# Linear attention in a deeper pipeline with scores in four row groups, and softmax attention with values of two tiles in one run, probabilities scaled by VectorE and scores of heads two and two

## The chip, the cores and the metric

The kernel runs on one core of a Trainium2 chip. Its time is the device time of one launch in microseconds (us), the median of three runs. The engines of the core are named as the profile names them: PE (TensorE; PEld is its loading of weights), DVE (VectorE), ACT (ScalarE), POOL (GpSimd) and SP (the queue of DMAs).

## What is computed

Two layers on x of shape (2, 1024, 256), in fp32. The first is linear attention with 16 heads of 16 features, computed in pieces of 64 positions by the reference (in tiles of 128 by the kernel). The second is a block of causal softmax attention (32 query heads, 8 key/value heads of 64) and a mixture of 8 experts, two for each token.

```
x = x + layernorm(linear_attention(layernorm(x)))
    # q, k: products of two feature maps; s = tril(q k^T); o = s v + q (sum of k^T v so far); o / rms(o)
y = layernorm(x)
h = y + attention(rmsnorm(y))        # softmax(q k^T / 8, causal) v, then wo
x = x + layernorm(h + moe(rmsnorm(h)))
```

## The kernel before

Each engine has its program written out by hand, in order, and semaphores join them: an engine that waits holds up everything behind it on that engine. Three stages follow each other.

**Stage 1, linear attention.** `pair_step(s, front, back)` works on tile s of both batches at once, 128 positions each, 8 tiles. Its front part turns normalised x (`xn` to `xnT`), makes four feature maps (L1109), q and k, the values, and the masked scores of tile s (`score`, L1120). Its back part, in the next step, makes the output of the tile before (L1131 state part, L1133 score part, in four column groups of 32), its rms, the projection `ao` (L1177), two layernorms and `rT_all`. For the scores the heads share 128 partitions, 16 each: POOL (L457) and ACT (L582) copy q eight times, each copy masked to one head (`qx`), and PE multiplies all 128 rows of k with 512 columns of them. DVE multiplies the result with the triangle (`mask`, L774).

**Stage 2, softmax attention.** A sequence is one key/value head of one batch; there are 16, and each has 8 query tiles of 128 (t is the tile's number over all, 128 in all; below c = t modulo 8, so tile c has w = 128(c+1) keys and c+1 blocks of 128 keys). For each tile and each of its four query heads PE makes scores (`score`, L1285 and L1286, two passes in fp32r), DVE adds the causal mask, writes the result to `probs` and takes the row maximum (`maximum`, L884), ACT exponentiates and sums (`exponent`, L640). In the next step PE transposes the probabilities block by block (L1301, four heads to a block, into three PSUM banks used in turn, `TURNS`), and ACT and DVE take turns in copying the blocks out (`evacuate_part`, L648 and L892). One step later `values` (L1313) multiplies them with the values into `bank[2]`, in two column groups. The row sums are turned to the other layout by a copy on POOL (`spread`, L500) and two transposes (L1298); DVE divides by them when it takes the output (`oT`, L909). Then comes `project_out` (L1322) and the sum into `acc` (L922). `project` makes one of six slices of keys, values and queries (L1253) or a transpose of the values (L1243) at the end of each step; ACT and DVE split its result (L630 to L634, and `low_part`, L872 and L877).

**Stage 3** routes the tokens and runs 39 slots of experts (L1401, L1410).

The order of stage 2 on PE is this, for each t from 0 on (`third` splits the blocks of a tile in three parts):

```
score(t,0)  values(t-2)  score(t,1)  turn_part(t-1,0)  score(t,2)  turn_part(t-1,1)
project_out(t-2)  score(t,3)  turn_part(t-1,2)  project(item_of(t))
```

## Time and profile before

| | |
|---|---|
| median of 3 runs | 1934.72 us (1933.41 to 1934.87) |
| the profiled execution: its time, its span | 1933.22 us, 1931.3 us |
| busy in the span: PE, PEld, DVE, ACT, POOL | 94%, 74%, 55%, 48%, 14% |
| TensorE clock granted, mean | 0.976 of full speed |
| chain that ended last: PE, DVE, ACT | 86%, 7%, 2% |

The span runs from the first to the last instruction. A matmul's row gives its whole duration, and following matmuls begin before it ends, so the pace of PE is read from the starts of two rows.

### The profile page before, as it was taken

What the parts mean: (1) busy time and instruction counts of PE and PEld (TensorE: products, weight loads), DVE (VectorE), ACT (ScalarE), POOL (GpSimd) and SP (SyncE); (2) the same over time, 40 slices, a digit from 0 to 9 for tenths busy, and PEclk for the clock granted to TensorE, in tenths of its full rate; (3) what the DMA queues carried; (4) which work ended last, traced back from release to release, by engine and by line L of the source; (5) the groups of instructions that cost most, each with busy time, mean ns of one, the idle gap of its engine ahead of it and who ended that gap; (6) DMA issues with size and microseconds to landing.
All of it is one profiled execution on the core that took longest, in us unless ns stands there. A gap on an engine that the chain in (4) does not pass through costs nothing.

```text
span 1931.3 us, 32217 instructions
## 1 busy us (share of the span) xinstructions
PE 1813.6 (94%) x12286; PEld 1428.7 (74%) x12286; DVE 1055.0 (55%) x2465; ACT 924.1 (48%) x2049; POOL 261.1 (14%) x355
## 2 busy tenths in 40 slices
PE   6999689999999999999999999999985999999994
PEld 5666457777777777777777777777765999999993
DVE  3666556766776766767767667667655111111112
ACT  3343255655656656656656656656651222222223
POOL 2222110000000000000000000000001222222222
PEclk9999889999999999999999999999986999999997
DMA  2000010000000000000000000000017134213443
GB/s 83 0 0 0 0 44 1 9 1 1 9 1 1 9 1 1 10 1 1 9 1 1 9 1 1 1 1 1 23 34 245 22 92 128 48 26 87 119 125 95
DMA packets 46042, 60.02 MB, mean 31 GB/s; under 512 B 8944, under 2 KB 39536, under 8 KB 45936
## 3 DMA queue, kind: packets, MB, share of 16 engines
q1 hardware_dynamic: 36336, 46.16, 7.2%
q0 software_dynamic: 7536, 10.36, 3.2%
q10 hardware_dynamic: 2064, 2.10, 0.3%
q8 instruction: 66, 1.08, 0.2%
q14 instruction: 40, 0.33, 0.1%
HBM read 138.43 MB, written 11.40 MB: 78 GB/s over the span
## 4 chain that ended last, share of the span: by engine, by line
PE 86%; DVE 7%; ACT 2%; issue 2%; POOL 1%; DMA 1%; SPq 0%; DVEq 0%; POOLq 0%; ACTq 0%
PE wide L1401 15%; PE bank L1313 13%; PE bank L1301 12%; PE bank L1253 9%; PE wide L1285 8%; PE bank L1410 7%; PE wide L1286 7%; PE bank L1322 6%; PE wide L1120 2%; PE bank L1109 2%; PE bank L1298 1%; ACT qhl L634 1%; PE bank L1177 1%; DVE arena L802 1%; PE bank L1243 1%
## 5 line engine op out<-in xcount | busy, mean ns | idle before, releaser
L884 DVE CUSTOM_DVE_ANT_0 arena<-wide,arena 128x896 f32<-128x896 f32 (+7 forms) x512 | 383.8, 755 | 223.2 <-PE wide L1286 219.3
L640 ACT ACTIVATE arena<-arena,nmax 128x896 f32<-128x896 f32 (+7 forms) x512 | 397.0, 776 | 177.3 <-DVE nmax L884 174.2
L1285 PE MATMUL wide<-khi,qhl 128*128 128x512 f32 (+3 forms) x768 | 346.3, 452 | 1.7 <-DVE qhl L877 1.7
L1301 PE MATMUL bank<-ident,arena 128*128 128x128 f32 x2304 | 308.5, 274 | 0.0
L648 ACT COPY arena<-bank 128x512 f32<-128x512 f32 (+1 forms) x352 | 191.7, 545 | 214.0 <-PE bank L1301 206.3
L1401 PEld LDWEIGHTS wide<-wo,arena 128*128 128x128 f32 x2496 | 287.0, 193 | 3.2 <-issue 1.3
L1401 PE MATMUL wide<-wo,arena 128*128 128x128 f32 x2496 | 287.3, 277 | 0.9 <-ACT wo L693 0.9
L1313 PE MATMUL bank<-arena,vt 128*64 128x256 f32 x2304 | 277.0, 385 | 0.0
L1301 PEld LDWEIGHTS bank<-ident,arena 128*128 128x128 f32 x2304 | 262.3, 141 | 16.6 <-issue 0.4
L1286 PE MATMUL wide<-klo,qhl 128*128 128x512 f32 (+3 forms) x768 | 256.0, 347 | 0.0
L1050 DVE TENSOR_TENSOR wo<-wide,wo 128x512 f32<-128x512 f32 x78 | 53.9, 692 | 368.1 <-PE wide L1401 368.1
L892 DVE COPY arena<-bank 128x512 f32<-128x512 f32 (+1 forms) x352 | 222.9, 639 | 9.2 <-PE bank L1301 8.4
L1313 PEld LDWEIGHTS bank<-arena,vt 128*64 128x64 f32 x2304 | 154.2, 137 | 90.8 <-issue 19.9
L1285 PEld LDWEIGHTS wide<-khi,qhl 128*128 128x128 f32 x768 | 145.3, 189 | 89.3 <-issue 65.6
L1286 PEld LDWEIGHTS wide<-klo,qhl 128*128 128x128 f32 x768 | 146.2, 190 | 36.9 <-issue 22.5
L500 POOL COPY arena<-rinv 128x256 f32<-128x256 f32 x128 | 51.0, 398 | 784.4 <-DVE rinv L905 782.4
L1322 PE MATMUL bank<-wo,oT 128*128 128x256 f32 x512 | 135.1, 387 | 11.3 <-DVE oT L909 11.3
L1410 PE MATMUL bank<-arena,wo 128*128 128x256 f32 x624 | 141.2, 380 | 0.0
L703 ACT ACTIVATE wo<-wide 128x512 f32<-128x512 f32 x78 | 46.6, 597 | 170.3 <-PE wide L1401 170.3
L1410 PEld LDWEIGHTS bank<-arena,wo 128*128 128x128 f32 x624 | 115.8, 191 | 13.9
L1253 PE MATMUL bank<-rT_all,wq_g 128*128 128x512 f32 x256 | 122.5, 602 | 0.3
L1322 PEld LDWEIGHTS bank<-wo,oT 128*128 128x128 f32 x512 | 87.3, 191 | 24.3 <-DVE oT L909 14.7
(221 smaller groups left out, 1749.8 us busy)
## 6 DMA issues: line engine op xcount, KB each, us to landing
arena<-in_L_ffn_w SPq DMA_DIRECT2D x117, 1024.0 KB
x_all<-in_L_attn_x ACTq DMA_DIRECT2D x1, 2048.0 KB, 9.9
wq_g<-in_L_ffn_wq SPq DMA_DIRECT2D x8, 256.0 KB, 3.5
wo<-in_L_ffn_wo SPq DMA_DIRECT2D x16, 128.0 KB, 3.0
hbuf<-acc SPq DMA_DIRECT2D x2, 1024.0 KB, 4.6
tbuf<-rT_all SPq DMA_DIRECT2D x4, 512.0 KB, 3.0
acc<-hbuf SPq DMA_DIRECT2D x4, 512.0 KB, 5.5
out<-x_all SPq DMA_DIRECT2D x8, 256.0 KB, 2.1
```

The lines of the kernel that those rows point to most:

```text
L640: nc.scalar.activation(probs[t % 2][:, h, 0:w], probs[t % 2][:, h, 0:w], ACT.Exp, bias=nmax[:, t % 2, h:h + 1], scale=-1.0, accum_out=rsum ...
L648: nc.scalar.copy(*turned_to(t, m)).then_inc(S("pT_even"), 1)
L884: nc.vector.tensor_tensor_reduce(out=probs[t % 2][:, h, 0:w], in0=score_bank(t, h)[:, 0:w], in1=causal[:, SEQ - w:SEQ], scale=-1.0, scalar ...
L892: nc.vector.tensor_copy(*turned_to(t, m)).then_inc(S("pT_odd"), 1)
L1253: ins = mm(to, w, rT_all[:, k, at:at + HALF], start=(k == 0), stop=(k == KB - 1))
L1285: mm(dst, q, khi[:, lo:lo + cols], start=True, stop=False)
L1286: ins = mm(dst, q, klo[:, lo:lo + cols], start=False, stop=True)
L1301: ins = nc.tensor.transpose(to[:, h * P:(h + 1) * P], probs[t % 2][:, h, m * P:(m + 1) * P], ident[:])
L1313: ins = mm(bank[2][u * DH:(u + 1) * DH, 0:2 * P], vt[:, n % 2, m], pT[t % 2][m][:, u * 2 * P:(u + 1) * 2 * P], start=(m == 0), stop=(m == ct))
L1322: ins = mm(bank[2][:, 2 * P:2 * P + D], oT[:, j], wo2[:, t // (BATCH * TB), j], start=(j == 0), stop=(j == 1))
L1401: ins = mm(wide[:, at + half, f * P:(f + 1) * P], w[:, k, (half * 4 + f) * P:(half * 4 + f + 1) * P], sT[u][:, k], start=(k == 0), stop=(k ...
L1410: ins = mm(bank[u][:, 0:D], gated[:, f], w2_e[u][:, f], start=(f == 0), stop=(f == FB - 1))
```

## The change

**Stage 1.** `qx` holds two copies of q in place of eight: `rowmask` marks, in each group of 32 partitions, the two heads that live there. PE multiplies 32 rows of k with 256 columns, in four row groups (`ROWS`), each with a bank of its own, for both batches in one `score(k)`. POOL masks with one instruction a step instead of two, ACT with two instead of eight. The steps are written out instead of looped, and reach over four steps: the masks 2 and 3 of a tile are at the head of the next step, its layernorms one step later, and its last transposes (`rn`) another one later. POOL takes the additions to `state` and to x; ACT takes normalising x and a copy `aos` of the projection.

**Stage 2.** `spread` and its transposes are gone. DVE scales `probs` in place by one over the row sum (`normalise`, four instructions a tile, with a reciprocal for each pair of heads), and the transposes of a tile wait for all four. ACT alone copies the transposed blocks out. `values` runs in even steps only, for tiles t-3 and t-2 together; ACT copies its result, and `project_out` takes both tiles into one of the three banks, after which DVE adds both to `acc` in one instruction. PE makes the scores of heads 0 and 1 one after the other, and those of 2 and 3. ACT's order is `exponent(t,0)`, in even steps the copy of `oT`, then as before.

The core of the diff:

```
-            for t in range(TILES + 2):
-                scored, turning, weighing = t < TILES, 1 <= t <= TILES, t >= 2
+            for t in range(STEPS):
+                scored, turning = t < TILES, 1 <= t <= TILES
                 if scored:
                     score(t, 0)
-                if weighing:
-                    values(t - 2)
-                if scored:
                     score(t, 1)
+                if weighed_in(t):
+                    values(t)
                 if turning:
                     turn_part(t - 1, 0)
+                    turn_part(t - 1, 1)
                 if scored:
                     score(t, 2)
-                if turning:
-                    turn_part(t - 1, 1)
-                if weighing:
-                    project_out(t - 2)
-                if scored:
                     score(t, 3)
+                if weighed_in(t):
+                    project_out(t)
                 if turning:
                     turn_part(t - 1, 2)
...
+            def normalise(t, h):
+                w = (t % TB + 1) * P
+                if h % 2 == 0:
+                    invert(t, h // 2)
+                    v.wait_ge(S("rinv_ready"), 2 * t + h // 2 + 1)
+                nc.vector.tensor_scalar(probs[t % 2][:, h, 0:w], probs[t % 2][:, h, 0:w], rinv[:, t % 2, h:h + 1], None, ALU.mult).then_inc(S("probs_ready"), 1)
...
                 if scored:
                     maximum(t, 0)
+                if turning:
+                    normalise(t - 1, 2)
+                    normalise(t - 1, 3)
                 if item:
                     low_part(item)
...
                 if scored:
                     maximum(t, 2)
+                    normalise(t, 0)
...
                     maximum(t, 3)
+                    normalise(t, 1)
...
-                        pe.wait_ge(S("exp_done"), G * (t + 1))
+                        pe.wait_ge(S("probs_ready"), G * (t + 1))
...
-                    for j in range(2):
-                        ins = mm(wide[:, 2 * b + j, :], kT[:, k, b], qx[:, k, b, j * 4:(j + 1) * 4].rearrange("p h c -> p (h c)"), start=True, stop=True)
+                    for b in range(BATCH):
+                        for j in range(ROWS):
+                            rows = slice(j * P // ROWS, (j + 1) * P // ROWS)
+                            ins = mm(wide[:, j, b * HR * P:(b + 1) * HR * P], kT[rows, k, b], qx[rows, k, b].rearrange("p h c -> p (h c)"), start=True, stop=True)
```

How the instructions stand now. On PE, the step c = 7 of a sequence (L1285 and L1286 are the two passes of the scores, L1313 values, L1301 transposes of probabilities, L1322 the projection), before:

```order
L1285 MATMUL wide<-khi,qhl 128x512
L1286 MATMUL wide<-klo,qhl 128x512
L1285 MATMUL wide<-khi,qhl 128x512
L1286 MATMUL wide<-klo,qhl 128x512
L1313 MATMUL bank<-arena,vt 64x256 x12
L1285 MATMUL wide<-khi,qhl 128x512
L1286 MATMUL wide<-klo,qhl 128x512
L1285 MATMUL wide<-khi,qhl 128x512
L1286 MATMUL wide<-klo,qhl 128x512
L1301 MATMUL bank<-ident,arena 128x128 x8
```

and after the change, its second half and the beginning of step c = 0 (L1305 and L1306 are the scores, L1316 the transposes, L1330 the values):

```order
L1316 MATMUL bank<-ident,arena 128x128 x12
L1263 MATMUL bank<-ident,vT 128x64 x4
L1305 MATMUL wide<-khi,qhl 128x128
L1306 MATMUL wide<-klo,qhl 128x128
L1305 MATMUL wide<-khi,qhl 128x128
L1306 MATMUL wide<-klo,qhl 128x128
L1330 MATMUL bank<-arena,vt 64x256 x26
L1316 MATMUL bank<-ident,arena 128x128 x20
```

The values of step 7 have moved to the even step, where 13 blocks (26 matmuls) run at once; five blocks are transposed in one run behind them.

On DVE, in the step c = 7, before (L884 the maximum, L877 `low_part`, L892 copies of transposed blocks, L922 the sum into `acc`):

```order
L884 ISA arena,nmax<-wide,arena 128x1024
L884 ISA nmax 128x1
L877 SCALAR_TENSOR_TENSOR qhl<-bank,qhl 64x512 x2
L905 RECIPROCAL rinv<-rsum 128x4
L909 TENSOR_TENSOR oT<-bank,arena 128x256
L884 ISA arena,nmax<-wide,arena 128x1024
L884 ISA nmax 128x1
L892 COPY arena<-bank 128x512
```

and after (L908 the maximum, L916 `normalise`, L901 `low_part`):

```order
L908 ISA arena,nmax<-wide,arena 128x1024
L908 ISA nmax 128x1
L921 RECIPROCAL rinv<-rsum 128x2
L916 TENSOR_SCALAR arena<-arena,rinv 128x896 x2
L901 SCALAR_TENSOR_TENSOR qhl<-bank,qhl 64x512 x2
L908 ISA arena,nmax<-wide,arena 128x1024
L908 ISA nmax 128x1
L908 ISA arena,nmax<-wide,arena 128x1024
```

The scaling of heads 2 and 3 of the tile before now stands behind the first maximum of this tile, ahead of `low_part`.

## Rows read from the trace of the kernel before

**Rows 1.** The page's busy times, whole run.

```profile
PE 1813.6 (94%) x12286; PEld 1428.7 (74%) x12286; DVE 1055.0 (55%) x2465; ACT 924.1 (48%) x2049; POOL 261.1 (14%) x355
```

**Rows 2.** Busy by stretch: from:to and length, PE, PEld, DVE, ACT, POOL, clock.

```profile
23.50:245.80 222.30, 194.79 (x1452) 136.84 (x1453) 134.19 (x230) 81.09 (x192) 49.26 (x41) 0.97 0.00 0
245.80:1428.00 1182.20, 1165.21 (x7421) 856.93 (x7422) 817.11 (x1951) 718.52 (x1570) 91.14 (x194) 1.00 0.02 6
1428.00:1931.30 503.30, 445.30 (x3368) 427.17 (x3368) 94.88 (x242) 117.12 (x276) 114.79 (x88) 0.93 0.35 98
```

**Rows 3.** Chain that ended last: start, length, what, count; two steps, two sequences.

```profile
155.60 2.01 PE bank L1177 x8
...
181.26 2.01 PE bank L1177 x8
...
591.69 2.31 PE bank L1313 x20
...
665.13 2.31 PE bank L1313 x20
```

**Rows 4.** PE's timeline in step c = 7: start, busy, line, shapes, count.

```profile
676.09 0.39 PE L1285 MATMUL wide<-khi,qhl 128*128 128x512 f32 x1
676.32 0.40 PE L1286 MATMUL wide<-klo,qhl 128*128 128x512 f32 x1
676.64 2.81 PE L1313 MATMUL bank<-arena,vt 128*64 128x256 f32 x24
679.38 0.50 PE L1285 MATMUL wide<-khi,qhl 128*128 128x512 f32 x1
679.72 0.39 PE L1286 MATMUL wide<-klo,qhl 128*128 128x512 f32 x1
...
681.21 0.48 PE L1285 MATMUL wide<-khi,qhl 128*128 128x512 f32 x1
...
682.21 1.47 PE L1301 MATMUL bank<-ident,arena 128*128 128x128 f32 x12
683.52 1.03 PE L1322 MATMUL bank<-wo,oT 128*128 128x256 f32 x4
```

**Rows 5.** Groups by form in one sequence, 591.69 to 665.13 us: busy, mean ns.

```profile
L648 ACT COPY arena<-bank 128x512 f32<-128x512 f32 x18 | 10.5, 584 | 13.2 <-PE bank L1301 12.9
...
L1253 PE MATMUL bank<-rT_all,wq_g 128*128 128x512 f32 x16 | 7.6, 600 | 0.0
...
L884 DVE CUSTOM_DVE_ANT_0 arena<-wide,arena 128x1024 f32<-128x1024 f32 x4 | 4.9, 1225 | 3.2 <-PE wide L1286 3.2
L640 ACT ACTIVATE arena<-arena,nmax 128x1024 f32<-128x1024 f32 x4 | 4.6, 1151 | 1.0 <-DVE nmax L884 1.0
...
L884 DVE CUSTOM_DVE_ANT_0 arena<-wide,arena 128x512 f32<-128x512 f32 x4 | 2.7, 685 | 1.6 <-PE wide L1286 1.6
```

**Rows 6.** DVE's groups by form, whole run.

```profile
L892 DVE COPY arena<-bank 128x512 f32<-128x512 f32 x288 | 196.5, 687 | 8.5 <-PE bank L1301 8.4
...
L819 DVE TENSOR_SCALAR arena<-bank,mv,rstd 128x256 f32<-128x256 f32 x16 | 8.0, 539 | 6.5 <-POOL rstd L443 6.5
L783 DVE TENSOR_SCALAR arena<-x_all,hmean,hrstd 128x256 f32 x14 | 5.1, 406 | 0.0
...
L739 DVE TENSOR_SCALAR gate<-gate,ln 128x8 f32<-128x8 f32 x2 | 0.4, 228 | 1.7 <-DMA gate<-in_L_ffn_gate_w 1.7
```

**Rows 7.** Groups by line, whole run, of stage 1.

```profile
L1120 PE MATMUL wide<-arena,wo 128*128 128x512 f32 x128 | 59.5, 599 | 7.7 <-DVE arena L774 7.7
...
L774 DVE TENSOR_TENSOR arena<-wide,tri 128x1024 f32<-128x1024 f32 x32 | 39.2, 1224 | 11.7 <-PE wide L1120 11.7
L582 ACT ACTIVATE arena<-wo,headmask 128x256 f32<-128x256 f32 x64 | 26.3, 497 | 0.0
...
L1120 PEld LDWEIGHTS wide<-arena,wo 128*128 128x128 f32 x128 | 22.5, 190 | 33.1 <-issue 19.6 <-DVE arena L774 13.5
...
L1133 PE MATMUL bank<-arena 128*32 128x128 f32 x512 | 19.8, 273 | 0.0
```

More of the change, by code:

```diff
@@ L553, in pair_step @@
+            def pair_step(s):
+                front, mid, back, last = s < TB, 1 <= s <= TB, 2 <= s <= TB + 1, 3 <= s
                 if front:
                     act.wait_ge(S("xnT_psum"), s + 1)
-                    if back:
+                    if s:
                         act.wait_ge(S("v_psum"), s)
                     nc.scalar.copy(whole(xnT[:]), bank[3][:]).then_inc(S("xnT_ready"), 1)
-                if back:
+                if last:
+                    act.wait_ge(S("rT_psum"), s - 2)
+                    for k in range(KB):
+                        ins = nc.scalar.activation(rT_all[:, k].rearrange("p (b t c) -> p b t c", b=BATCH, t=TB)[:, :, s - 3],
+                                                   bank[1][:, k * BATCH * P:(k + 1) * BATCH * P].rearrange("p (b c) -> p b c", b=BATCH), ACT.Copy, scale=ln1[:, k:k + 1])
+                    ins.then_inc(S("rT_ready"), 1)
+                if front:
+                    act.wait_ge(S("q1_psum"), s + 1)
+                    if s:
+                        act.wait_ge(S("qT_ready"), s)
+                    nc.scalar.activation(whole(q1s), bank[0][:], ACT.Identity, bias=fbias_q[:, 0:1], scale=DK ** -0.5).then_inc(S("q1_ready"), 1)
+                if mid:
@@ L616, in _ @@
             act.wait_ge(S("ln_loaded"), 16 * (2 * KB + 1))
-            pair_step(0, True, False)
-            with act.Fori(1, TB) as s:
-                pair_step(s, True, True)
-            pair_step(TB, False, True)
+            normal_x(0)
+            for s in range(TB + 3):
+                pair_step(s)
             def evacuate(item):
@@ L659, in _ @@
                     exponent(t, 0)
+                if weighed_in(t):
+                    n = 2 * P * len(weighed_in(t))
+                    act.wait_ge(S("o2_psum"), t // 2)
+                    nc.scalar.copy(oT[:].rearrange("p x j c -> p (x j c)")[:, 0:n], bank[2][:, 0:n]).then_inc(S("oT_ready"), 1)
                 if turning:
@@ L801, in pair_step @@
                 if back:
-                    nc.vector.reciprocal(halves[0][:, 1], halves[1][:, 1]).then_inc(S("orstd_ready"), 1)
-                    v.wait_ge(S("orstd_ready"), s)
-                    nc.vector.tensor_tensor(whole(onT), bank[2][:], orstd[:], ALU.mult).then_inc(S("onT_ready"), 1)
+                    v.wait_ge(S("x1_ready"), i)
+                    variance(i, xb, "x1")
+                if mid:
+                    v.wait_ge(S("oms_ready"), s)
+                    for k in range(KB):
+                        ins = nc.vector.reciprocal(halves[0][:, k], halves[1][:, k])
+                    ins.then_inc(S("orstd_ready"), 1)
                 if front:
@@ L1096, in _, with pair_step @@
             pe.wait_ge(S("wfeat_ready"), 4)
-            def pair_step(s, front, back):
+            def pair_step(s, front, mid, last):
                 def turn(to, src, given):
@@ L1170, in pair_step @@
                     feature(bank[1], 3, "k2_psum")
-                if back:
+                    if mid:
+                        pe.wait_ge(S("oms_ready"), s)
+                    for b in range(BATCH):
+                        for k in range(KB):
+                            ins = mm(bank[3][:, b * D:(b + 1) * D], xnT[:, k, b], wvT[:, k], start=(k == 0), stop=(k == KB - 1))
+                    ins.then_inc(S("v_psum"), 1)
+                    pe.wait_ge(S("kT_ready"), s + 1)
+                    turn(bank[1], lambda k, b: kT[:, k, b], "ktok_psum")
+                    score(0)
+                if mid:
                     pe.wait_ge(S("onT_ready"), s)
@@ L1200, in pair_step @@
                     ins.then_inc(S("kv_psum"), 1)
[L1201 to L1211 removed]
+                    score(1)
+            for s in range(TB + 3):
+                pair_step(s, s < TB, 1 <= s <= TB, s >= 3)
             pe.wait_ge(S("rT_ready"), TB)
@@ new lines, in turn_part, with values @@
+                    for h in range(G):
+                        ins = nc.tensor.transpose(to[:, h * P:(h + 1) * P], probs[t % 2][:, h, m * P:(m + 1) * P], ident[:])
+                    ins.then_inc(S("pT_psum"), 1)
+            def values(s):
+                if s > 2:
+                    pe.wait_ge(S("oT_ready"), s // 2 - 1)
+                for x, t in enumerate(weighed_in(s)):
+                    n, ct = divmod(t, TB)
+                    for m in range(ct + 1):
+                        pe.wait_ge(S("pT_ready"), blocks_before(t) + m + 1)
+                        if m == ct and ct % (TB // 2) == 0:
+                            pe.wait_ge(S("v2_ready"), 2 * n + 1 + ct // (TB // 2))
+                        for u in range(2):
+                            ins = mm(bank[2][u * DH:(u + 1) * DH, x * 2 * P:(x + 1) * 2 * P], vt[:, n % 2, m], pT[t % 2][m][:, u * 2 * P:(u + 1) * 2 * P],
+                                     start=(m == 0), stop=(m == ct))
```

427 lines of the change are left out of this document (191 added, 236 removed).

## Prediction

> **What bounds the kernel now.** I read the page's busy times first: PE is busy for 94% of the span [rows 1]. A busy PE need not be at its pace, so next come the stretches. Stage 1 takes 222 us, stage 2 1182 us, stage 3 503 us [rows 2]. The change leaves stage 3 alone, and it costs the same in the sum. In stage 2 the other engines are busy for 817 (DVE) and 719 us (ACT) of 1182. The chain of waits gives the periods: the same matmul comes back after 25.66 us in stage 1 (one step) and after 73.44 us in stage 2 (one sequence of 8 tiles) [rows 3]. So what the change is worth is read from 7 steps and 16 sequences.
>
> **PE's work in a sequence.** The prices are distances between starts in PE's timeline. A block of transposes (4) takes 0.435 us (12 in 1.31 us), a block of values 0.43 (24 matmuls in 2.74 us, less some 0.15 for the change of shape), the scores of a head of 1024 keys 1.00 (681.21 to 682.21); for fewer keys I take them in proportion, with 0.12 at 128 [rows 4]. A projection of keys or queries is four matmuls at 0.43 each, 1.72 us: such a pass of 512 columns lasts 600 ns where one of the scores lasts 0.39 us and has a distance of 0.23, so 0.21 more [rows 4, 5]. The output projection of a tile is four of half that, 0.86. That gives, for 36 blocks and 32 heads: transposes 15.7, values 15.5, scores 16.9, projections 10.3, output 6.9, the two transposes of `spread` for each tile 1.7, and the transposes of vT 1.2 (an estimate: 8 short ones, and a change of shape before and behind each four). Each run of values costs more beside that: it begins 0.32 us behind the scores' last pass where the pass itself takes 0.23, its own first pair is late by 0.15, and the scores behind it need 0.34 where 0.23 would do [rows 4]. That is 0.35, with scatter 0.38, 8 times: 3.0. The sum is 71.2 of 73.4 us. PE stands still for 2.2 us in a sequence, no more: stage 2 is bound by PE's work.
>
> **What stage 2 loses.** The `spread` transposes go: -1.7 us. Four of the 8 runs of values go: -1.5. The work of PE is then 68.0 us. If nothing made it wait, stage 2 would win up to 5.4 us a sequence, 86 us in all.
>
> **What stage 2 gains in waits.** The scaling of `probs` is not in the trace. The nearest rows are those of the same instruction: with two scalars and 256 columns it takes 539 ns out of PSUM and 406 ns out of SBUF [rows 6]. DVE's full pace is 1.05 ns a column (1225 against 685 ns for 512 columns more) [rows 5], so the PSUM form is 267 + 272, and the SBUF form 134 + 272: half the time for a column. With one scalar and 8 columns it is 228 ns, 220 of them fixed. I take 0.22 us + 0.52 ns a column: 0.75 us at 1024, 0.69 at 896, 0.49 at 512, and as the other bound the full pace, 1.29 at 1024.
>
> Now follow an odd step, c = 7, from the start of its first scores. PE needs 1.9 us for heads 0 and 1 and then wants to transpose tile c = 6, but no values stand between, since they run in even steps. The transposes wait for all four scalings of that tile, and two of them stand on DVE behind this tile's first maximum. The first head's scores end at 0.93, their result is there at 1.13 (a matmul's end comes some 0.2 after the next begins), the maximum takes 1.24 with its read-out, to 2.37, the reciprocal with its own wait 0.2, the two scalings 1.3 (the second overlaps the first a little), the semaphore 0.1: the transposes begin at 4.0, 2.1 after PE is free. The same sum gives 1.8 for c = 5, 1.5 for c = 3 and 0.7 for c = 1: 6.1 us in a sequence. In even steps the runs of values (2.2 to 5.6 us) cover this chain.
>
> The second wait is for PSUM banks. Before, ACT and DVE took turns in copying, and a copy lasts 0.58 us on ACT and 0.69 on DVE against 0.435 for the transposes of a block [rows 4, 5, 6]. Now ACT copies all 36 blocks of a sequence between 32 exponentials, which last up to 1.15 us, 1.24 with the sum's read-out. ACT's work is 719 / 16 = 45 us a sequence now; 18 more whole copies and 4 of `oT` make it 58, less some 2 for the half copies of `spread`. DVE's is 51; it gives up 18 whole copies (12.4 us), the half ones and the scaling of `oT`, and gets 32 scalings of 0.52 (16.6) and more reciprocals: 50 to 55 us [rows 2, 5, 6]. Neither is the bound by its sum, but the order is strict. In step 7, ACT makes two copies to 5.9, the exponential of head 1 (whose maximum stands on DVE behind the two scalings and 1.4 us of `low_part`, and ends at 6.5) to 7.8, two copies to 9.0, the exponential of head 2 to 10.2, and then the first of the last three copies, to 10.9. PE's vT transposes want the bank of that one. By then PE would have been ready at 9.4, so the step ends near 11.3 us where its work is 7.4. I went through the other steps in the same way, each beginning where the last left the three engines. Work and end for c = 0 to 7 come out as 13.4/14.2, 3.1/3.8, 10.0/10.0, 3.8/5.3, 10.2/11.0, 6.7/8.7, 13.7/13.8, 7.4/11.3. The even steps lose up to 0.8, where PE wants a bank whose `acc` sum or copy is late, or where the scores of c = 4, which take two banks a head, wait for the maximum of c = 3's head 3. The sum is 78.1 us. Rounding down for overlaps that I left out, I take 77.9: **+4.5 us a sequence, 16 times, +72 us.** The waits behind DVE's order are certain in this order and set a floor of 68.0 + 6.1 = 74.1, +0.7 a sequence or +11 us; the bank waits (3.8 us) are the uncertain part. With the full pace for the scalings each odd step gets about 0.5 worse, and DVE is busy for 65 us: +8 a sequence, +130 us, is the upper bound.
>
> **Stage 1.** The masked scores are 16 passes of 512 columns a step at 0.43 us: 6.9 of 25.66 us [rows 3, 7]. The new form is 32 passes of 256 columns on 32 rows. If four row groups run at once, they take 32 x 0.215 / 4 = 1.7 us; if one after the other, 6.9 as before. The trace shows no row groups. The nearest row is the output part in column groups: 512 matmuls of 128 columns are busy for 19.8 us, 39 ns each, where alone each would need 54 or more [rows 7], so groups of the array do overlap. The loads of weights are the limit between: a load with 128 columns and the pass behind it follow each other every 0.109 us in the transposes [rows 4], and 32 of those are 3.5 us. I take 3.4 for the scores, -3.5 us a step.
>
> The Trainium skill, in "TensorE: Matmul & The Clock Gate", section "LDWEIGHTS (loading the stationary operand)", says that a load costs its columns over 1.2 GHz whatever its rows: by that an estimate of 32 x 107 ns, 3.4 us. The same page's table of packed matmuls has four row tiles 3.07 times as fast, by which the scores would take 2.2 us and stage 1 would win 8 us more. No run here shows either yet.
>
> The rest of a step's 25.66 us is 15.8 us of other PE work and 3 us in which PE waits: for the masks (the chain of L774, 1.22 us each, four a step, 7.7 us of waits in all) [rows 7], for `kT` and for `xn`. In the new order I find masks and reciprocals still late by 1 to 1.5 us. ACT's eight masking instructions (0.50 us each) become two, with two copies more; that lies beside PE. POOL's one instruction instead of two, and its two additions, lie beside PE too. A step comes out at 19 to 20 us, -6 each, -42 for seven; the first step wins 4 to 5 us, and the end of the pipeline, where the last tile's chain runs alone over three steps, stays within some us of its 25. **Stage 1: -46 us**, with -10 (row groups one after the other) and -60 as bounds.
>
> **The sum:** 1933.2 (the profiled execution: 1931.3 of span and 1.9 around it) - 46 + 72 = 1959. The median of the runs lies 1.5 us higher, so 1960 us. A change of under 0.2% (4 us) can't be told from none with this kernel's runs.
>
> **The rivals.**
> Banks not a limit: the waits for ACT's copies vanish in the slack of the even steps, and only DVE's order costs. What speaks for it: ACT has over 12 us of slack in a sequence. Against it: ACT's order puts exponentials between copies just in the tiles with most blocks. Stage 2 +11 to +20, the whole near 1900 to 1908. This is the case on the other side; it decides when the bank waits are under some 2 us a sequence instead of 3.8. Chance 0.22.
> PE unhindered: DVE and ACT run ahead, stage 2 wins 40 to 86 us and the whole is 1800 to 1850. Against it stands the position of the two scalings behind the first maximum. Chance 0.08.
> Row groups do nothing: the scores of stage 1 run one after the other, -10 instead of -46, the whole near 1996. The column groups speak against it. Chance 0.10.
> DVE or ACT becomes the bound: scalings at full pace, or more held up behind them than I followed, stage 2 +110 to +130, the whole 2000 to 2020. For it: DVE's and ACT's work would be 55 to 65 us in 78, in strict order. Chance 0.14.
>
> **How the numbers follow.** My own case, with stage 2 at +50 to +95, has 0.46 and its own range is 1930 to 1985. The range 1893 to 2015 takes in the first rival and most of the third and fourth, and leaves out some 0.1 below and 0.06 above. Faster: the two rivals on that side, 0.30. Within 0.2%: 0.07, between my case and the first rival. Slower: 0.63.
>
> **What would show it.** Of the profile after: the distance of the same matmul of two sequences (77.9, against 74.1 or 68); PE's idle time ahead of the transposes, put down to the scalings on DVE, some 100 us in all; idle time ahead of vT's transposes or of the last third of transposes, put down to ACT's copies; the scalings' mean of 0.52 us; the step of stage 1 at 19 to 20 us, and the pace of its scores' passes, 0.05, 0.11 or 0.21 us. I'd be wrong if the odd steps had no idle time ahead of the transposes, or if stage 1 won under 20 us.

## The result and the profile after

| | before | after |
|---|---|---|
| median | 1934.07 us (1932.27 to 1934.87, 4 runs) | 1974.65 us (1972.35 to 1976.14, 4 runs) |
| ratio, 95% interval | | 1.0209 [1.0194, 1.0224] |
| profiled span | 1931.3 us | 1970.3 us |

The change makes the kernel slower by 2.1%. The page's busy times after:

```profile
PE 1759.3 (89%) x12158; PEld 1414.0 (72%) x12158; DVE 1021.9 (52%) x2547; ACT 1056.8 (54%) x2314; POOL 208.0 (11%) x236
```

PE's share falls from 94 to 89% [rows 1], 1813.6 to 1759.3 us of busy time: PE works less and waits more. The stretches after (from:to and length, then busy time of PE, PEld, DVE, ACT, POOL, and the granted clock) are stage 1 and stage 2:

```profile
23.50:206.70 183.20, 159.52 (x1584) 127.02 (x1584) 114.59 (x201) 73.52 (x169) 46.01 (x48) 0.95 0.01 1
206.70:1474.00 1267.30, 1151.56 (x7203) 856.61 (x7203) 806.66 (x2068) 861.53 (x1863) 40.26 (x66) 0.98 0.02 6
```

The chain that ended last (start, duration, what). The first two rows are the same matmul in two steps of stage 1, the third is stage 2's first projection, the others are the values of step c = 0 in three sequences in a row:

```profile
103.14 2.00 PE bank L1134 x8
...
122.74 2.00 PE bank L1134 x8
...
206.71 7.47 PE bank L1273 x12
...
676.68 5.76 PE bank L1330 x52
...
755.27 5.76 PE bank L1330 x52
...
832.73 5.76 PE bank L1330 x52
```

A step of stage 1 takes 19.60 us where it took 25.66, and stage 2 begins at 206.71 instead of 245.80 [rows 2]: stage 1 wins 39.1 us. A sequence takes 78.59 and then 77.46 us, where it took 73.44 [rows 3]; the rest of the run is 78.1 us longer, from there to the span's end. 78.1 less 39.1 is the 39.0 by which the span grew. Why one sequence is 1.1 us shorter than its neighbours is taken up below; the distances of the 14 from 283.43 to 1382.28 are 77.4 to 77.5 twice and 78.6 to 78.9 twelve times.

The groups after that answer to [rows 5, 6], from the page (busy, mean ns | idle before and what ended it):

```profile
L908 DVE CUSTOM_DVE_ANT_0 arena<-wide,arena 128x896 f32<-128x896 f32 (+7 forms) x512 | 383.1, 753 | 341.8 <-PE wide L1306 338.0
L1316 PE MATMUL bank<-ident,arena 128*128 128x128 f32 x2304 | 318.2, 286 | 90.2 <-DVE arena L916 88.9
L683 ACT COPY arena<-bank 128x512 f32<-128x512 f32 x576 | 312.8, 585 | 112.3 <-PE bank L1316 111.8
L916 DVE TENSOR_SCALAR arena<-arena,rinv 128x896 f32<-128x896 f32 (+7 forms) x512 | 258.0, 525 | 9.1
```

and those of the scores on row groups, from the groups by form, which answer to [rows 7]:

```profile
L1146 PE MATMUL wide<-arena,wo 32*128 32x256 f32 x256 | 18.3, 400 | 1.5 <-DVE arena L819 1.5
L1146 PEld LDWEIGHTS wide<-arena,wo 32*128 32x128 f32 x256 | 11.6, 184 | 4.1 <-issue 3.0
```

The waits of the whole run (us in total, times, longest):

```profile
PE bank L1316 <- DVE arena L916: 88.9, 65, 2.0
...
DVE acc L948 <- PE bank L1342: 71.8, 64, 6.0
...
PE bank L1263 <- ACT arena L683: 12.6, 15, 0.9
...
PE wide L1305 <- DVE nmax L908: 9.6, 17, 0.6
```

PE waits 88.9 us ahead of the transposes (L1316) for the scalings (L916), in 65 places: four in each of 16 sequences. It waits 12.6 us ahead of vT's transposes (L1263) for ACT's copies, 0.84 in each sequence, and 9.6 us ahead of scores (L1305) for a maximum, 0.58 in the step c = 4 of each. Now step c = 7 in the sequence from 676.68 to 755.27 (timeline: start, duration, engine; idle before in brackets):

```profile
742.31 0.80 PE L1305 MATMUL wide<-khi,qhl 128*128 128x512 f32 x1
...
743.84 1.23 DVE L908 CUSTOM_DVE_ANT_0 arena<-wide,arena 128x1024 f32<-128x1024 f32 x1 [1.40 <-PE wide L1306]
...
745.19 1.28 DVE L916 TENSOR_SCALAR arena<-arena,rinv 128x896 f32<-128x896 f32 x2
...
746.50 1.39 DVE L901 SCALAR_TENSOR_TENSOR qhl<-bank,qhl 64x512 fp32r<-64x512 f32 x2
...
746.62 3.55 PE L1316 MATMUL bank<-ident,arena 128*128 128x128 f32 x16 [1.91 <-DVE arena L916]
```

Read it downwards: DVE waits for the first scores, takes the first maximum (743.84) and, behind a reciprocal, two scalings (745.19 to 746.47). PE has finished its scores by 744.7 and stands still for 1.91 us. Then 16 transposes take 3.55 us, where 12 took 1.31 before the change [rows 4]. The stretches around that place, and around the same place one sequence later, show why (the last three numbers are clock, DMA share and GB/s):

```profile
744.70:746.60 1.90, 0.01 (x1) 0.01 (x1) 1.83 (x6) 1.24 (x2) 0.00 (x0) 1.00 0.00 0
746.60:750.20 3.60, 3.58 (x17) 3.60 (x18) 2.52 (x4) 2.18 (x3) 0.00 (x0) 0.53 0.00 0
...
823.30:825.20 1.90, 0.03 (x1) 0.00 (x0) 1.83 (x6) 1.24 (x2) 0.00 (x0) 1.00 0.00 0
825.20:828.80 3.60, 3.30 (x22) 2.87 (x23) 2.70 (x5) 2.06 (x3) 0.00 (x0) 1.00 0.02 5
```

After the same 1.90 us of standing still, the clock fell to its lower level (1.2 GHz, the mean of the stretch is 0.53) in one sequence and stayed at 2.4 GHz in the next. The low clock covers the transposes and ends with them. In the undisturbed sequence the same blocks go in two runs, the second behind a bank that DVE's `low_part` (L901) still reads:

```profile
825.24 1.06 PE L1316 MATMUL bank<-ident,arena 128*128 128x128 f32 x8 [1.90 <-DVE arena L916]
826.57 1.09 PE L1316 MATMUL bank<-ident,arena 128*128 128x128 f32 x8 [0.27 <-DVE qhl L901]
...
831.68 0.46 PE L1263 MATMUL bank<-ident,vT 64*128 64x64 f32 x4 [0.85 <-ACT arena L683]
```

The last row is the end of the step: vT's transposes wait 0.85 us for ACT's copy, as they do in each sequence. From its first scores to those of the next step, c = 7 takes 11.13 us there and 12.29 with the lower clock. Of the 15 sequences with such a step 13 have such a piece. By the mean distance of 78.49 against 77.46 it costs 1.0 us a sequence, some 15 of the 78 us.

### The profile page after: what moved, and what is told of

Same layout as the page of the kernel before. It is cut to its first block, busy times and chain, and to the rows that moved or that the text cites. A ratio compares the mean times of both kernels' runs of the same rounds, so it can differ in the third digit from the quotient of the medians.

```text
span 1970.3 us, 31548 instructions
## 1 busy us (share of the span) xinstructions
PE 1759.3 (89%) x12158; PEld 1414.0 (72%) x12158; DVE 1021.9 (52%) x2547; ACT 1056.8 (54%) x2314; POOL 208.0 (11%) x236
## 4 chain that ended last, share of the span: by engine, by line
PE 81%; DVE 13%; ACT 3%; issue 1%; DMA 1%; POOL 1%; SPq 0%; POOLq 0%; DVEq 0%
PE wide L1418 14%; PE bank L1330 13%; PE bank L1316 12%; PE bank L1273 9%; PE bank L1427 7%; PE bank L1342 6%; PE wide L1305 5%; PE wide L1306 5%; DVE arena L908 5%; DVE arena L916 3%; PE bank L1134 3%; ACT arena L676 2%; DVE qhl L901 2%; PE wide L1146 1%; PE bank L1216 1%
## 5 line engine op out<-in xcount | busy, mean ns | idle before, releaser
L908 DVE CUSTOM_DVE_ANT_0 arena<-wide,arena 128x896 f32<-128x896 f32 (+7 forms) x512 | 383.1, 753 | 341.8 <-PE wide L1306 338.0
L1316 PE MATMUL bank<-ident,arena 128*128 128x128 f32 x2304 | 318.2, 286 | 90.2 <-DVE arena L916 88.9
L1316 PEld LDWEIGHTS bank<-ident,arena 128*128 128x128 f32 x2304 | 268.5, 146 | 151.1 <-issue 132.0
L683 ACT COPY arena<-bank 128x512 f32<-128x512 f32 x576 | 312.8, 585 | 112.3 <-PE bank L1316 111.8
L1305 PE MATMUL wide<-khi,qhl 128*128 128x512 f32 (+3 forms) x768 | 312.2, 414 | 11.3 <-DVE nmax L908 9.6
L1330 PE MATMUL bank<-arena,vt 128*64 128x256 f32 x2304 | 263.0, 382 | 0.0
L916 DVE TENSOR_SCALAR arena<-arena,rinv 128x896 f32<-128x896 f32 (+7 forms) x512 | 258.0, 525 | 9.1
L1306 PE MATMUL wide<-klo,qhl 128*128 128x512 f32 (+3 forms) x768 | 254.4, 349 | 0.0
L1330 PEld LDWEIGHTS bank<-arena,vt 128*64 128x64 f32 x2304 | 159.8, 137 | 84.2 <-issue 8.4
L1305 PEld LDWEIGHTS wide<-khi,qhl 128*128 128x128 f32 x768 | 148.5, 193 | 53.5 <-DVE nmax L908 19.9
L1306 PEld LDWEIGHTS wide<-klo,qhl 128*128 128x128 f32 x768 | 148.0, 193 | 36.7 <-issue 22.5
L506 POOL CAST khi<-khi 64x512 fp32r<-64x512 f32 x32 | 19.5, 609 | 1100.8 <-ACT khi L666 1100.8
L698 ACT COPY oT<-bank 128x512 f32<-128x512 f32 (+1 forms) x65 | 37.8, 581 | 169.4 <-PE bank L1330 169.4
L1342 PE MATMUL bank<-wo,oT 128*128 128x256 f32 x512 | 123.3, 383 | 0.6 <-ACT oT L698 0.6
```

The lines of the kernel that those rows point to most:

```text
L683: nc.scalar.copy(pT[t % 2][m], bank_of((t, m))).then_inc(S("pT_ready"), 1)
L908: nc.vector.tensor_tensor_reduce(out=probs[t % 2][:, h, 0:w], in0=score_bank(t, h)[:, 0:w], in1=causal[:, SEQ - w:SEQ], scale=-1.0, scalar ...
L916: nc.vector.tensor_scalar(probs[t % 2][:, h, 0:w], probs[t % 2][:, h, 0:w], rinv[:, t % 2, h:h + 1], None, ALU.mult).then_inc(S("probs_rea ...
L1305: mm(dst, q, khi[:, lo:lo + cols], start=True, stop=False)
L1306: ins = mm(dst, q, klo[:, lo:lo + cols], start=False, stop=True)
L1316: ins = nc.tensor.transpose(to[:, h * P:(h + 1) * P], probs[t % 2][:, h, m * P:(m + 1) * P], ident[:])
```

## The experiments

"Sequence" is the distance of the same matmul in two sequences. Each ratio is against the kernel before on the same chip; that one took 1932.0 to 1934.1 us on the chips used, so a difference between two experiments is good to some 2 us.

**Stage 1 alone.** Stage 1 of the change, stage 2 as before: the loop of PE, DVE and ACT over stage 2's steps is the old one.

```
-            for t in range(STEPS):
-                scored, turning = t < TILES, 1 <= t <= TILES
+            for t in range(TILES + 2):
+                scored, turning, weighing = t < TILES, 1 <= t <= TILES, t >= 2
```

> Stage 1 of the changed kernel with stage 2 of the kernel before. The two kernels' traces put stage 1 at 39.5 us less (first scores of stage 2 at 215.4 instead of 254.9 us) and stage 2 at some 79 us more. If the stages are independent, this kernel takes 1934 - 39 = 1895 us, with 73.4 us a sequence and 19.6 us a step. Rival: the gain of stage 1 is tied to the new stage 2 (the clock, or the hand-over between the stages), then it is less than 30 us.

Measured: 1892.21 us, ratio 0.9792 [0.9776, 0.9808], sequence 73.47 us, as the theory had it. The two stages don't touch one another: stage 1 wins 40 us, so stage 2 loses some 82 (1974.65 - 1892.21).

**Scalings first.** The two late scalings go ahead of the first maximum, nothing else.

```
-                if scored:
-                    maximum(t, 0)
                 if turning:
                     normalise(t - 1, 2)
                     normalise(t - 1, 3)
+                if scored:
+                    maximum(t, 0)
```

> The changed kernel with the two scalings of heads 2 and 3 of the tile before ahead of this tile's first maximum on DVE. Theory: of the 2 us that PE waits ahead of the transposes in step 7 the maximum (1.24) and the wait for this tile's first scores go, unless the exponential of head 3 is late; odd steps get 0.5 to 1.2 us shorter, the waits for the scalings fall from 89 us to under 50, 75.5 to 77.5 us a sequence, 1925 to 1957 us. Rival (the exponential of head 3 comes too late, and DVE stands still instead): no gain or a loss, 1970 us or more.

Measured: 1907.36 us, 0.9869 [0.9853, 0.9886]; sequence 74.0 us, less than the theory's 75.5 to 77.5. Moving two instructions wins 67 of the 82 us: 3.5 us in each sequence (77.46 - 74.0), some 52 us, by the order, and the other 15 by the clock. Its chain and its waits on PE:

```profile
575.13 5.76 PE bank L1330 x52
...
649.13 5.76 PE bank L1330 x52
```

```profile
PE bank L1316 <- DVE qhl L901: 21.1, 15, 1.4
...
PE bank L1263 <- ACT arena L683: 12.6, 15, 0.8
```

The row of waits for the scalings, 88.9 us before, is gone from the top; what stays is in step c = 7. Its timeline there:

```profile
713.07 1.28 DVE L916 TENSOR_SCALAR arena<-arena,rinv 128x896 f32<-128x896 f32 x2
...
714.27 1.22 DVE L908 CUSTOM_DVE_ANT_0 arena<-wide,arena 128x1024 f32<-128x1024 f32 x1
...
714.49 1.06 PE L1316 MATMUL bank<-ident,arena 128*128 128x128 f32 x8
...
715.52 1.39 DVE L901 SCALAR_TENSOR_TENSOR qhl<-bank,qhl 64x512 fp32r<-64x512 f32 x2
...
716.97 1.12 PE L1316 MATMUL bank<-ident,arena 128*128 128x128 f32 x8 [1.41 <-DVE qhl L901]
```

The scalings now lie beside PE's scores, and the transposes begin as soon as PE is free. The next wait appears at once: two blocks later PE wants the bank that `low_part` on DVE still reads. That is a bank wait, but DVE's, not ACT's; the one for ACT's copy ahead of vT's transposes stays as it was (12.6 us). In c = 4 the scores now wait 1.03 us for a maximum where it was 0.58. So of the 5.5 us of waiting that go, 3.5 are won. The gaps of 1.9 us are gone, and with them each fall of the clock in stage 2 (1.00 from 265 to 1370 us).

**No scaling.** All scalings and reciprocals are left out, and the transposes wait for the exponentials.

```
-                if turning:
-                    normalise(t - 1, 2)
-                    normalise(t - 1, 3)
...
-                    normalise(t, 0)
...
-                    normalise(t, 1)
...
-                        pe.wait_ge(S("probs_ready"), G * (t + 1))
+                        pe.wait_ge(S("exp_done"), G * (t + 1))
```

> The changed kernel without the scaling of the probabilities and its reciprocals (left out of the computation); the transposes wait for the exponentials. Theory: the 6 us a sequence of waits ahead of the transposes in odd steps shrink to those for the exponential of head 3, under 2 us, and the waits for ACT's copies stay, 2 to 4 us: 71 to 74 us a sequence, 1870 to 1905 us. Rival (ACT's copies are the true bound and take over): 76 us or more, over 1935 us.

Measured: 1872.69 us, 0.9688 [0.9672, 0.9704]; sequence 72.16 us. Stretches of stage 2 without its ends, of this kernel, of the one with the scalings first, of the change and of the kernel before, in this order:

```profile
265.00:1370.00 1105.00, 1074.04 (x6895) 796.49 (x6894) 508.04 (x1225) 811.13 (x1766) 35.33 (x58) 1.00 0.01 4
```
```profile
265.00:1370.00 1105.00, 1050.90 (x6697) 773.38 (x6695) 749.53 (x1929) 793.72 (x1731) 36.55 (x58) 1.00 0.01 4
```
```profile
265.00:1370.00 1105.00, 1006.74 (x6296) 751.34 (x6295) 708.01 (x1814) 753.93 (x1632) 34.15 (x56) 0.98 0.01 3
```
```profile
265.00:1370.00 1105.00, 1092.16 (x6979) 804.38 (x6977) 768.66 (x1835) 674.64 (x1475) 84.29 (x180) 1.00 0.02 4
```

PE is busy for 97.2, 95.1, 91.1 and 98.8% of it. Without scalings a sequence has 70.1 us of busy PE (0.972 of 72.16) and 2.0 of waiting; before it was 72.6 of 73.45. So the change's real saving of PE's work is 2.5 us a sequence by busy time, and even a free scaling would win 1.3 us of distance only. The sequence lies in the theory's range, but the waits for ACT's copies are 0.84 us of the 2.0 and not 2 to 4; 0.96 are for the bank that `low_part` reads.

**Heads apart.** PE scores the heads one at a time, with transposes and values between, in the order S0 V S1 T0 S2 T1 O S3 T2 instead of S0 S1 V T0 T1 S2 S3 O T2.

```
                 if scored:
                     score(t, 0)
-                    score(t, 1)
                 if weighed_in(t):
                     values(t)
+                if scored:
+                    score(t, 1)
                 if turning:
                     turn_part(t - 1, 0)
-                    turn_part(t - 1, 1)
                 if scored:
                     score(t, 2)
-                    score(t, 3)
+                if turning:
+                    turn_part(t - 1, 1)
                 if weighed_in(t):
                     project_out(t)
+                if scored:
+                    score(t, 3)
```

> The changed kernel with PE's scores in the old places: head 1 behind the values, head 2 between the two first parts of the transposes, head 3 behind the projection. Theory (the transposes wait for two scalings that stand behind the first maximum, and ACT alone copies): the odd steps keep both waits, so the sequence stays at 78.6 within 1.5 us, 1975 us within 20. Rival (scores two and two are what costs): it falls by 3 us a sequence or more, to 1925 or less.

Measured: 1942.02 us, 1.0050 [1.0033, 1.0066]; sequence 76.5 us, the waits for the scalings as long as ever (87.9 us in 64 places). That is 0.6 us below the range of the theory, and far from the rival's 3 us.

Step by step, c = 4 takes 10.02 us instead of 11.03. The rest sums to what it is in the undisturbed sequences of the change (77.46), c = 7 with 11.13 too. The other half of the gain is the clock: with this order it fell in four sequences only, with the same gaps, and cost 0.35 us each time. Pairing the heads itself costs 1.0 us a sequence.

**Third head first.** `score(t, 2)` goes ahead of the transposes.

```
+                if scored:
+                    score(t, 2)
                 if turning:
                     turn_part(t - 1, 0)
                     turn_part(t - 1, 1)
                 if scored:
-                    score(t, 2)
                     score(t, 3)
```

> The changed kernel with PE's scores of head 2 ahead of the transposes, where PE stands still in odd steps. Theory: the wait ahead of the transposes takes in up to 1 us of scores, so the waits for the scalings fall by some 40 to 60 us of 89 and the sequence to 75 to 77.5 us, 1915 to 1957 us. Rival (the end of the step is set by ACT's copies, so work moved into the gap only lengthens the wait behind it): the wait for ACT grows and the sequence stays within 1 us of 78.6.

Measured: 1960.93 us, 1.0148 [1.0131, 1.0166]; sequence 77.73 us. The waits for the scalings fall by 55 us, as the theory had it, but the sequence does as the rival said. More than half of what went stands under another name now:

```profile
PE bank L1316 <- DVE arena L916: 33.7, 64, 0.8
PE wide L1305 <- DVE nmax L908: 31.5, 63, 1.0
```

These two rows make 65.2 us where they were 98.5. The rest came back as busy time: PE is busy for 72.1 us of an undisturbed sequence, where it was 70.2. Why its work takes longer in this order isn't shown. Against 77.46 it wins nothing. What this kernel is ahead of the change, 14 us by the medians, is mostly the clock's: with gaps of at most 1.0 us it fell in two sequences of 16, at 1.7 us each, where in the change it fell in 13 of 15.

**Copies shared.** DVE copies each third transposed block, ACT two of three.

```
-                    act.wait_ge(S("pT_psum"), j + 1)
-                    nc.scalar.copy(pT[t % 2][m], bank_of((t, m))).then_inc(S("pT_ready"), 1)
+                    if j % 3 != 2:
+                        act.wait_ge(S("pT_psum"), j + 1)
+                        nc.scalar.copy(pT[t % 2][m], bank_of((t, m))).then_inc(S("pT_act"), 1)
...
+                    if j % 3 == 2:
+                        v.wait_ge(S("pT_psum"), j + 1)
+                        nc.vector.tensor_copy(pT[t % 2][m], bank_of((t, m))).then_inc(S("pT_dve"), 1)
```

> The changed kernel with every third transposed block copied by DVE, each behind the next maximum. Theory: waits for banks shrink (3.8 us a sequence by the walk through the steps), DVE gets 12 copies of 0.69 us a sequence more, of which some stand ahead of a maximum or a scaling: 75 to 78 us a sequence, 1918 to 1965 us. Rival (banks no limit, DVE is): 80 us or more, over 1995 us.

Measured: 1977.86 us, 1.0233 [1.0216, 1.0251]; sequence 78.2 us with the clock up, 79.4 with a fall: between the theory and the rival. The wait for ACT ahead of vT's transposes is gone, and one for DVE's copies (L927) has come:

```profile
PE bank L1335 <- DVE arena L927: 17.3, 32, 0.6
```

In c = 7 PE now waits 0.57 us for DVE's copy, and the step ends at 11.12 us where it ended at 11.13; c = 5 takes 9.22 instead of 8.48. So taking a third of ACT's copies away wins nothing. It doesn't show that PE never waits for ACT, as it does for 0.84 us a sequence; it shows that DVE is no better place for them.

**No scaling and copies shared.** Both edits together; the scaling is left out as above.

> No scaling (left out of the computation), and every third block copied by DVE. With no scaling alone the sequence is 72.2 us, of PE's work of 68.0. Theory: most of the remaining 4.2 us are waits for banks that ACT alone copies; they fall to under 2, 69 to 70.5 us a sequence. Rival (they are changes of shape and waits for the sum into acc or for maxima): 71.5 us or more.

Measured: 1879.75 us, 0.9729 [0.9713, 0.9745]; sequence 72.6 us, 0.45 more than with ACT's copies alone, as the rival had it. (Its 68.0 us of PE's work were my estimate; the trace has 70.) DVE is busy for 56% of stage 2 (619.9 of 1105 us), and sharing still doesn't pay: 0.84 us of waiting for ACT go, 1.09 for DVE's copies come.

**Sum behind the last maximum.** The sum into `acc`, which on DVE waits 71.8 us for PE, goes behind `maximum(t, 3)`.

```
+                if scored:
+                    maximum(t, 3)
...
-                    maximum(t, 3)
```

> The changed kernel with DVE's sum into acc behind the maximum of head 3 instead of ahead of it. Heads apart won 1.0 us in step 4 and 1.1 in step 7 of each sequence. Theory A: pairing costs since head 3's scores then come ahead of the projection while its maximum still waits behind the sum that needs it; then this edit wins most of the same, 76.5 to 77.5 us a sequence, 1940 to 1957 us. Theory B: it costs in odd steps, through the order of heads 2 and 3 against the transposes: the sequence stays at 78 to 79, and DVE's wait for the projection alone falls.

Measured: 1976.10 us, 1.0219 [1.0202, 1.0236]. The wait falls to 39.4 us, the sequence is 77.73 us with the clock up (79.0 and 78.9 with a fall). Theory B holds: a DVE wait of 72 us that costs nothing is slack.

**Scalings first and third head first.** Both edits, to see whether the second is worth something once the scalings are early.

> The scalings ahead of the first maximum (74.0 us a sequence by itself) and the score of the third head ahead of the transposes (77.7 us by itself). With the scalings early the transposes have nothing to wait for, so that the third score ahead of them only waits for the maximum of head 0 to release its banks, with the transposes queued behind it. Theory A, that one early piece of work is enough and the third score does harm once the scalings are early: 75 to 77 us a sequence, 1925 to 1955 us. Theory B, that both orders gain apart from one another (0.9 us a sequence by the run of the third score alone): 73.1 us and 1893 us.

Measured: 1923.05 us, 0.9949 [0.9932, 0.9965]; sequence 74.8 us. Theory A holds, with a little less harm than it had: one early piece of work is enough, and the second costs 0.8 us a sequence.

**Scalings first and heads apart.**

> The two scalings go ahead of the first maximum on VectorE (as in the run with the scalings first, 74.0 us a sequence, where the changed kernel has 78.6) and TensorE scores the heads one by one with transposes or values between them (as in the run with the heads apart, 76.5). Theory A, that the late scalings and the pairing are two separate losses: the gains add except in the step with 7 blocks, where both act on the same stall; a sequence of 72 to 73 us, and 1875 to 1895 us, with the step with 4 blocks at 10.5 us where the run with the scalings first has 11.8. Theory B, that pairing only hurts because the scalings are late (nothing then fills the wait of the third score): with the scalings first it costs nothing more, a sequence stays at 74 us and the time at 1905 us. At 72 us a sequence it would be ahead of the kernel with stage 1 alone (1892 us), at 74 behind it.

Measured: 1893.89 us, 0.9797 [0.9781, 0.9814]; sequence 73.42 us. The gain over 74.0 is 0.6, between the two theories: with the scalings early, pairing costs 0.6 instead of 1.0. The stage 2 of the change, in its best order, is just as long as the one before (73.44), so this kernel ends level with the one of stage 1 alone. I found no version that beats 1892 us with the computation whole.

**Row groups in turn.** Stage 1 alone, with the scores' loop over row groups outside.

```
-                    for b in range(BATCH):
-                        for j in range(ROWS):
+                    for j in range(ROWS):
+                        for b in range(BATCH):
```

> Stage 1 of the change with stage 2 as before (1892.2 us), and in stage 1's sixteen score matmuls the loop over row groups is outside and the one over batches inside, so that four matmuls in a row stand on the same row group and neighbours on different groups are rare. The matmuls, their sizes and their number are the same. Theory A, that the pace of 0.05 us a pass in the changed kernel comes from neighbours on different row groups running at once: the passes now follow one another at 0.1 to 0.2 us, a run of sixteen takes 1.7 to 3.3 us where it took 1.15, two runs of it and the loads add 1 to 4 us a step, and with eight steps the time is 1900 to 1920 us. Theory B, that the pace is that of a pass with 32 rows whatever stands beside it: 0.05 us again and 1892 us, within 0.2%.

**One row group.** Stage 1 alone, all scores from rows 0 to 31.

```
-                            rows = slice(j * P // ROWS, (j + 1) * P // ROWS)
+                            rows = slice(0, P // ROWS)
```

> As the kernel with stage 1 alone changed (1892.2 us), but all sixteen score matmuls of stage 1 read rows 0 to 31, so that no two of them stand on different row groups. This changes the computation: three quarters of stage 1's scores are those of the first eight heads' rows. The run with the row groups in turn kept a pace of 0.05 us a matmul with four neighbours on each group (sixteen in 1.17 us), and left open whether work on the four groups still overlapped. Theory A, that the groups overlap and a quarter-row pass by itself lasts longer: by the 0.215 us a pass that 256 columns take in the same stage with all rows, sixteen take 3.4 us, and 32 a step in eight steps add some 36 us, so 1928 us; by half of it, 1.7 us a run and 1902 us. Theory B, that a pass on 32 rows has that pace by itself, whatever its neighbours: 1.15 us a run of sixteen and 1892 us, within 0.2%.

Measured: in turn 1892.42 us, 0.9796 [0.9779, 0.9812]; one group 1951.51 us, 1.0094 [1.0078, 1.0111]. The chain of the one with stage 1 alone, of the one in turn and of the one on one group, all in the middle of stage 1:

```profile
113.63 1.08 PE wide L1142 x16
...
121.31 1.99 PE bank L1130 x8
...
140.90 1.99 PE bank L1130 x8
```
```profile
114.90 1.10 PE wide L1142 x16
```
```profile
135.48 3.65 PE wide L1142 x16
...
141.84 2.00 PE bank L1130 x8
...
166.57 1.99 PE bank L1130 x8
```

Sixteen passes take 1.08 us on four groups, 1.10 with four passes in a row on each group, and 3.65 on one. So it is the overlap of the groups that wins, not a short pass, and it doesn't need neighbours on different groups in the program's order. From the first start to the last it is 0.77, 0.79 and 3.34 us. Of the theories, the time in turn fits B, and the run on one group refutes B and bears out A's first half: the groups overlap, whatever the order. The step grows from 19.59 to 24.73 us, by twice 2.57. That is 36 to 41 us in seven or eight steps; the rest of the 59 is in the main in the first steps, where the clock was lower. Two stretches of the one on one group:

```profile
85.00:116.00 31.00, 30.33 (x196) 23.82 (x196) 14.19 (x25) 8.35 (x19) 5.68 (x7) 0.78 0.00 1
...
141.00:166.00 25.00, 24.76 (x203) 20.14 (x202) 14.46 (x26) 9.15 (x22) 5.64 (x6) 1.00 0.01 2
```

PE is busy for 98 and 99% in both, and yet the clock is 0.78 in the first. With the four groups it is 1.00 from 54 to 184 us. Why it fell here, with PE busy throughout, stays open.

## Why the prediction was right, and where it was not

The predicted 1960 us is 14.7 below what was measured. The direction held, and so did the chain of cause behind it. But the term for the bank waits was mis-sized, PE's work was priced too low by about as much, and one cause was missing. The steps of stage 2, from the first scores of a step to those of the next, read from the starts of PE's rows (with "clock up" in the sequence from 754.61 us, the others medians):

| step c | 0 | 1 | 2 | 3 | 4 | 5 | 6 | 7 | sum |
|---|---|---|---|---|---|---|---|---|---|
| predicted work | 13.4 | 3.1 | 10.0 | 3.8 | 10.2 | 6.7 | 13.7 | 7.4 | 68.3 |
| PE busy after, clock up | 13.63 | 3.29 | 9.90 | 4.24 | 10.43 | 6.90 | 13.73 | 8.11 | 70.2 |
| predicted end | 14.2 | 3.8 | 10.0 | 5.3 | 11.0 | 8.7 | 13.8 | 11.3 | 78.1 |
| after, clock up | 13.63 | 4.05 | 9.90 | 5.52 | 11.01 | 8.48 | 13.73 | 11.13 | 77.5 |
| after, with fall | 13.63 | 4.05 | 9.90 | 5.52 | 11.03 | 8.48 | 13.73 | 12.29 | 78.6 |
| scalings first | 13.63 | 3.11 | 9.90 | 4.46 | 11.46 | 7.38 | 13.71 | 10.34 | 74.0 |
| no scaling | 13.63 | 3.10 | 9.90 | 4.25 | 10.51 | 7.30 | 13.72 | 9.75 | 72.2 |

**The transposes wait for the scalings behind the first maximum** (6.1 us a sequence): right. The price of a scaling was 0.52 us by estimate and 0.525 by the trace, 0.751 at 1024 columns. The chain in c = 7 was to start the transposes 4.0 us behind the first scores with 2.1 of waiting; it was 4.3 and 1.91. The waits sum to 5.6 us a sequence (88.9 / 16). I called it a floor; the one swap of order proves it as cause, with 3.5 us of the sequence's distance at an even clock, and leaving the scalings out gives 5.3.

**The bank waits** (3.8 us, the "uncertain part"): over twice what they were. In a sequence with the clock up PE waits 7.2 us in all. Beside the 5.5 for the scalings there are 0.85 for ACT's copy ahead of vT's transposes, 0.27 for the bank that `low_part` reads and 0.58 for a maximum ahead of the scores of c = 4: 1.7 us, of which ACT's copies have half. The wait for ACT in c = 7 is of the kind that I had described, with 0.85 us where I had 1.5 (10.9 less 9.4), and the step ends at 11.13 us where I had 11.3. For the loss in c = 4 I had up to 0.8, and heads apart wins 1.0 there.

**PE's work** (68.0 us a sequence): too low by 2.2, which filled the place of the bank waits. So the agreement of 77.9 with 77.5 is in part luck: two errors of about 2 us cancelled. The larger part of this one lay in the kernel before. There PE is busy for 72.6 us of a sequence, where my prices gave 71.2 and 2.2 of standing still. One slip is in the sum: 1.00 us for a head of 1024 keys, in proportion to the keys, gives 18.0 us for the scores and not 16.9. The rest is the saving, 2.5 us by busy time and not 3.2. (Busy time takes in the end of the last matmul ahead of each wait, so it is a little more than the work; without scalings, where waits are few, it is 70.1.)

**The clock**: missing. The sum had the 1.9 us of standing still, but not that the transposes behind it may run at 1.2 GHz: 1.15 us in a step, some 15 us in the run. Without it the kernel would be near 1960 us, the forecast, with stage 1 some 7 us worse and stage 2 as much better than I had them (64 instead of 72 us).

**Stage 1** (-46 us): the step was right, 19.60 us. Within it two terms were off and cancelled. The row-group scores cost 2.16 us a step where I took the loads as the limit and 3.4, so they win 4.7 and not 3.5; the rest of the step then won 1.3 and not 2.5. The seven steps give the 42 us; the first step and the tail together lose 3 where I had them win 4. Which waits make up the 3 I didn't take apart.

The Trainium skill's load price ("TensorE: Matmul & The Clock Gate", "LDWEIGHTS (loading the stationary operand)") gives 16 x 107 ns, 1.7 us a run; the run takes 1.08, so here the measurement decides against it as a bound. The same page's table of packed matmuls has 3.07 times for four row tiles; here it is a little more, 3.65 / 1.08 or 3.4.

**The sum again:** 1933.2 - 39.1 + 78.1 = 1972.2, where I had -46 and +72; the profiled execution took 1972.35, and the median lies 2.3 above it instead of 1.5.

**The rivals.** "Banks not a limit" was to decide when the bank waits are under some 2 us a sequence. They are 1.7, so its condition came true. Its 1900 to 1908 us did not, since it stood on the same 68.0 us of work and knew nothing of the clock; that the run with the scalings first took 1907.36 has another cause. "Row groups do nothing" is refuted by the pace of the scores, 1.08 us for sixteen on four groups and 3.65 on one. "DVE or ACT becomes the bound": DVE's busy share in stage 2 is 64% and ACT's 68% (708 and 754 of 1105 us); the order is what costs, not the sum. "PE unhindered" failed at the position of the scalings, as argued.

## What to carry to other kernels

When work is moved from one engine to another, look where in the receiving engine's order it stands: two scalings of 0.65 us, one maximum too late, cost some 52 us, and the clock that fell behind the gaps 15 more; the cure was to move two lines. An engine that waits 72 us (DVE's sum) or does all of the copies (ACT) may have slack; an experiment that takes the suspect away is quicker than arguing. And when two orders are compared, compare their granted clock first: here it fell behind a gap of 1.9 us on TensorE in 13 of 15 sequences and cost 1.15 us each time. Last, a sum that comes out right can hide two terms that are wrong; compare the work and the waits apart.

## What the runs showed of the hardware

- In the change the clock fell to 1.2 GHz over the transposes (0.53 in the mean of 3.6 us) after PE had stood still for 1.9 us, in 13 of 15 sequences; the same gap left it at 2.4 GHz in the other two. With the same gap it fell in 4 of 15 with heads apart and in 4 of 15 with copies shared. In the run with the scalings first, where the longest wait of PE was 1.4 us, it stayed up throughout the middle of stage 2. But behind waits of at most 1.0 us it fell twice with the third head first, and twice more with that and the scalings first. So the length of the gap alone doesn't decide it; what does isn't shown.
- On one row group with PE busy for 98% of the stretch the clock was 0.78; on four groups 1.00.
- Passes of 256 columns on 32 rows: 16 in 1.08 us on four row groups, in 1.10 us with four in a row on each in the program's order, in 3.65 us on one. The last start 0.216 us apart, as do passes of 256 columns with all rows (L1130) in the same run: fewer rows alone win nothing.
